# A twelve-stage perceiver block: idle transposes at stage ends, first products by column group, tensors moved in parts, and a new order of rounds in the first cross-attention

## The chip, the cores and the metric

The kernel runs on one core of a Trainium2 chip. The metric is the device time of one execution in microseconds; the kernel before took 2767.07 us as a median of three runs (2764.23 to 2768.42).

## What is computed

The tokens x are 32 sequences of 64 positions with 128 features (2048 rows), the context is 32 sets of 1601 keys with 128 features. Twelve blocks are added to x in turn, each working on the normalised rows of x. The first:

```python
def _L0_xattn_ref(hm_tokens, text_tokens, text_mask, Wq, bq, Wk, bk, Wv, bv):
    Q = hm_tokens @ Wq + bq
    K = text_tokens @ Wk + bk
    V = text_tokens @ Wv + bv
    scores = jnp.einsum('bqd,bkd->bqk', Q, K) / jnp.sqrt(jnp.float32(d))
    scores = jnp.where(text_mask[:, None, :] == 0, jnp.float32(NEG), scores)
    attn = jax.nn.softmax(scores, axis=-1)
    return jnp.einsum('bqk,bkd->bqd', attn, V)
...
    x = x + _L0_xattn_ref(_layernorm(x, axis=-1), ctx_1024, mask_BxS2_ik0, ...)
    x = x + _L0_attn_ref(_layernorm(x, axis=-1), ...)   # and ten more blocks of this form
```

## The kernel before

x stays on the chip the whole time as 16 tiles of 128 rows by 128 features. Every block of the reference is one `Stage`; between two stages all engines meet at a barrier. Before the first there is `start` (L313), which reads x (1 MB, one transfer, L322) and the identity matrix `ident` (L323) and takes the row statistics of the 16 tiles (`measure` L165 with L169, `aggregate` L174 with L179); after the last there is `finish` (L340), which stores x to `out` in one transfer (L348).

**The normalisation.** Nearly every stage begins with the same three helpers. `ln_scalar` (L239) forms the standard deviation (L270); `ln_vector` (L190) its reciprocal (L206) and then the normalised tiles, 11 on VectorE (L213, `VECTOR_TILES` L161) and 5 on ScalarE (L252, `SCALAR_TILES` L162), in four groups of four tiles; the last group has two tiles on each. `ln_tensor` (L293) issues 14 transposes of the identity whose results nobody reads (L303, called idle transposes here) and then four transposes per group (L307), called PT0 to PT3. Their results are copied to `xnT` as four column groups T0 to T3: T0, T1 and T3 by ScalarE (L263), T2 by VectorE (L234). The two psum banks in `tp` alternate, so PT2 waits for T0 and PT3 for T1. The first products of each stage wait for T2 and T3, which means for all four groups.

**The first cross-attention** (`cross_attention`, L352 to L725, used once). SP issues all its transfers in one order: the mask (L428), six small weights (L430, the last, bv, L431), the context of round 0, then it waits until the mask has become additive keys on GpSimd (L486, L487), stores them to `scratch_q`, waits for that store, and reads them back spread over partitions as masks of rounds 0 to 2 (L446), with the contexts of rounds 1 to 3 between. One round r handles two of the 32 sequences: 1.6 MB of context are loaded (L437, L439); TensorE turns them, 26 transposes in 8 units T00 to T13 (L516), the first digit the sequence, the second the group of keys; ScalarE copies the T0 units (L702) and VectorE the T1 units (L641) to `ctxT`, which SP also stores for later stages (`context_turned`, 1.6 MB). The scores S0 to S3 (L540) go through mask and maximum on VectorE (L633, steps s0 to s3), the exponential on ScalarE (L710), four units of transposes of the probabilities p0 to p3 (L529), their copies (L722, and L682 for p3), 52 products with the context, M0 to M3 (L552), then division by the row sum (L660, step o), a transpose (L558, oT), its copy (L667), the product with Wv (L562, out) and the addition to x (L685), after which the tile's statistics for the next stage are taken. Round 0 also makes q (L505), qk (L570) and qbk (L573), and VectorE adds bv to all of x (L653) before it takes s0 of round 0.

The order on TensorE is written out by hand. In a steady round before it is T00 T10 T01, M0 M1 of round r-2, T11 T02 T12, M2 M3, S0, T03 T13, oT, p0 of round r-1, S1 to S3, p1 to p3, out. Three psum banks (`turn`) take the T and p units in turn, so each waits for the copy three units before it; `ctxT` and `sc` have two buffers, `ctx` four, the additive masks three. The fourth cross-attention (`kept_cross_attention`, L3790) is a separate function whose TensorE order has first the turns and then p, M and S of whole rounds.

## Time and profile before

The profiled execution took 2768.07 us; its span, from the first to the last instruction, is 2766.2 us, so 1.9 us lie around it. The mean clock granted to TensorE was 0.944 of full speed.

| stage | lines | from, us | to, us |
|---|---|---|---|
| start | 313 | 0 | 12.0 |
| first cross-attention | 352 | 12.3 | 223.5 |
| spectral | 1447 | 223.8 | 338.8 |
| capacity experts | 1671 | 339.1 | 453.4 |
| causal cross | 727 | 453.7 | 495.7 |
| two-step attention | 1183 | 496.0 | 665.4 |
| routed experts | 1911 | 665.7 | 923.3 |
| many-head cross | 3089 | 923.6 | 2053.1 |
| selective scan | 2166 | 2053.6 | 2311.6 |
| chosen adapters | 2561 | 2311.8 | 2401.6 |
| kept cross | 3790 | 2401.9 | 2569.7 |
| self-attention | 959 | 2570.0 | 2668.0 |
| quantised FFN | 2856 | 2668.3 | 2760.5 |
| finish | 340 | 2760.8 | 2766.2 |

How to read it: the stages follow each other without overlap, so a saving counts where it shortens a stage's longest chain. TensorE has two clock levels here, granted clock 1.0 (2.4 GHz) and 0.5 (1.2 GHz); the 14 idle transposes at a stage's start take 1.72 us at the first and 3.22 us at the second.

### The profile page before, as it was taken

The numbers are of one execution on the slowest core, as the hardware profiler recorded it, in microseconds if no ns is written. First come the engines' busy times: TensorE is split into PE (matmuls) and PEld (weight loads), VectorE is DVE, ScalarE is ACT, GpSimd is POOL, SyncE is SP. The second block draws the span as 40 slices with busy tenths as digits, with TensorE's granted clock in tenths as the row PEclk, the third lists the DMA queues.
The fourth block names the chain that finished last, engine by engine and source line by source line (L and its number), as shares of the span: only waits on it lengthen the run. The fifth ranks groups of instructions, "written<-read, shape, count | busy, mean of one in ns | idle before, by whom it ended". The sixth has DMA issues, their size and how long they took to land. (4 is left out here: it accounts for less than half of the span.)

```text
span 2766.2 us, 74345 instructions
## 1 busy us (share of the span) xinstructions
PE 2520.3 (91%) x31101; PEld 1693.8 (61%) x31101; DVE 1857.7 (67%) x6153; ACT 1385.0 (50%) x2566; POOL 433.1 (16%) x316
## 2 busy tenths in 40 slices
PE   7999844898999999999999999999987998899875
PEld 4776644455777556666666666666654554667544
DVE  5553423676211478888888888888857888466675
ACT  3443312565333245555555555555548994244452
POOL 1000022441000100000000000000002992056410
PEclk9999977998999789999999999999988999999987
DMA  6991041000000100000010000000001220298000
GB/s 213 336 309 36 23 153 41 10 3 18 16 16 16 33 25 26 26 26 26 26 35 29 26 26 26 26 26 26 15 10 57 99 92 16 72 344 285 10 2 16
DMA packets 73373, 181.12 MB, mean 65 GB/s; under 512 B 12130, under 2 KB 39717, under 8 KB 73008
## 3 DMA queue, kind: packets, MB, share of 16 engines
q1 hardware_dynamic: 72016, 174.52, 19.2%
q8 instruction: 247, 4.05, 0.6%
q0 software_dynamic: 1024, 1.85, 0.2%
q14 instruction: 86, 0.70, 0.1%
HBM read 145.80 MB, written 30.79 MB: 64 GB/s over the span
## 5 line engine op out<-in xcount | busy, mean ns | idle before, releaser
L3475 DVE CUSTOM_DVE_ANT_0 L_xattn_junk<-L_xattn_ps_mx,L_xattn_shift 128x512 f32<-128x512 f32 (+1 forms) x1024 | 545.0, 570 | 146.4 <-issue 145.8
L3553 ACT ACTIVATE L_xattn_pT<-L_xattn_ps_st 128x512 f32<-128x512 f32 x768 | 417.0, 595 | 322.6 <-PE L_xattn_ps_st L3290 204.8
L3305 PE MATMUL L_xattn_ps_mx<-L_xattn_kT,L_xattn_qb 32*128 32x512 f32 (+1 forms) x2048 | 530.2, 564 | 0.0
L3290 PE MATMUL L_xattn_ps_st<-L_xattn_qb,L_xattn_kT 32*128 32x256 f32 (+1 forms) x3328 | 462.9, 377 | 0.0
L3513 DVE TENSOR_TENSOR L_xattn_pT<-L_xattn_pT,L_xattn_capT 128x1024 f32<-128x1024 f32 (+1 forms) x324 | 360.1, 1113 | 7.7 <-ACT L_xattn_pT L3553 6.0
L3290 PEld LDWEIGHTS L_xattn_ps_st<-L_xattn_qb,L_xattn_kT 32*128 32x128 f32 (+1 forms) x3328 | 332.8, 181 | 7.1
L3355 PE MATMUL L_xattn_ps_pv<-L_xattn_pT,L_xattn_v 128*17 128x128 f32 x6656 | 261.6, 275 | 0.0
L3355 PEld LDWEIGHTS L_xattn_ps_pv<-L_xattn_pT,L_xattn_v 128*17 128x17 f32 x6656 | 148.6, 96 | 141.6 <-issue 124.5
L3305 PEld LDWEIGHTS L_xattn_ps_mx<-L_xattn_kT,L_xattn_qb 32*128 32x128 f32 x2048 | 176.5, 187 | 25.1 <-DVE L_xattn_tops L3475 18.9
L3317 PE MATMUL L_xattn_ps_st<-L_xattn_less,L_xattn_ones_b 3*128 3x512 bf16 x768 | 177.2, 385 | 0.0
L3228 POOL TENSOR_TENSOR L_xattn_qb<-ln_sq,L_xattn_four 128x256 f32<-128x256 f32 x32 | 20.6, 645 | 998.7 <-PE L_xattn_ps_st L3290 994.2
L2150 ACT ACTIVATE L_ffn_gelu<-L_ffn_ps_h,L_ffn_b 128x512 f32<-128x512 f32 x128 | 87.1, 688 | 130.7 <-PE L_ffn_ps_h L1999 127.4
L2122 DVE SCALAR_TENSOR_TENSOR x<-L_ffn_ps_o,L_ffn_weights,x 128x128 f32<-128x128 f32 x128 | 36.0, 345 | 169.4 <-PE L_ffn_ps_o L2009 169.4
L2009 PEld LDWEIGHTS L_ffn_ps_o<-L_ffn_w,L_ffn_gelu 128*128 128x128 f32 x1024 | 120.8, 194 | 16.6 <-issue 14.1
L3317 PEld LDWEIGHTS L_xattn_ps_st<-L_xattn_less,L_xattn_ones_b 3*128 3x128 bf16 x768 | 51.0, 91 | 130.0 <-ACT L_xattn_pT L3553 69.2
L2009 PE MATMUL L_ffn_ps_o<-L_ffn_w,L_ffn_gelu 128*128 128x128 f32 x1024 | 121.1, 277 | 1.9 <-DVE x L2122 1.9
L3376 PE MATMUL L_xattn_ps_prep<-L_xattn_wv,L_xattn_ctxT 128*32 128x128 f32 (+1 forms) x3264 | 117.8, 278 | 0.0
L1999 PE MATMUL L_ffn_ps_h<-xnT,L_ffn_w 128*128 128x512 f32 x256 | 117.0, 600 | 0.0
L3249 PE MATMUL L_xattn_ps_prep<-L_xattn_ctxT,L_xattn_wk 128*32 128x512 f32 x992 | 108.7, 510 | 0.0
L3887 POOL TENSOR_SCALAR L_xattn_out_keys<-L_xattn_mask 128x1536 bf16<-128x1536 uint8 x16 | 78.8, 4926 | 171.0 <-DMA L_xattn_rest<-context_turned 153.4
L2547 ACT ACTIVATE L_attn_xs<-L_attn_xiT,L_attn_bt 128x256 f32<-128x256 f32 x256 | 105.2, 494 | 0.0
L3376 PEld LDWEIGHTS L_xattn_ps_prep<-L_xattn_wv,L_xattn_ctxT 128*32 128x32 f32 (+1 forms) x3264 | 91.9, 111 | 15.5 <-ACT L_xattn_kT L3566 10.0
(633 smaller groups left out, 4853.9 us busy)
## 6 DMA issues: line engine op xcount, KB each, us to landing
L_xattn_ctx<-in_ctx SPq DMA_DIRECT2D x64, 768.0 KB
context_turned<-L_xattn_ctxT SPq DMA_DIRECT2D x32, 800.5 KB, 9.4
L_xattn_ctxT<-context_turned SPq DMA_DIRECT2D x32, 800.5 KB, 4.4
L_xattn_rest<-context_turned SPq DMA_DIRECT2D x32, 544.5 KB, 9.2
L_attn_cc<-scratch_rows SPq DMA_DIRECT2D x32, 512.0 KB, 3.6
L_xattn_out_keys<-scratch_q SPq DMA_DIRECT2D x32, 200.1 KB, 10.0
L_ffn_w<-in_L_ffn_w SPq DMA_DIRECT2D x4, 1024.0 KB, 9.4
L_ffn_w<-in_L_ffn_W SPq DMA_DIRECT2D x16, 256.0 KB, 3.1
```

What stands on the lines that cost most here:

```text
L1999: nc.tensor.matmul(ph[:, k, :], w1[:, e % 2, P * k:P * k + P], c.xnT[:, 512 * i:512 * i + 512], start=True, stop=True).then_inc(PE.did(f"h ...
L2009: last = nc.tensor.matmul(po[:, n % 2, P * j:P * j + P], g[:, n % 2, k, P * j:P * j + P], w2[:, e % 2, k, :], start=(k == 0), stop=(k == F ...
L2547: last = nc.scalar.mul(xs[:, k % 2, j, :], xiT[:, t, :], bt[:, t, n:n + 1])
L3249: last = nc.tensor.matmul(to[32 * q:32 * q + 32, 0:width], wk[:, 32 * q:32 * q + 32], ctxT[:, n % 2, 512 * m:512 * m + width], start=True, ...
L3290: last = nc.tensor.matmul(st[0:chunk[j], w % 3, 256 * c2:256 * c2 + 256], kT[n % 3][r:r + 32, P * j:P * j + chunk[j]], qb[n % 3][r:r + 32, ...
L3305: last = nc.tensor.matmul(mx[:, w % 3, to:to + width], qb[n % 3][32 * g:32 * g + 32, 2 * (p % 2):2 * (p % 2) + 2, :].rearrange("p h q -> p ...
L3317: nc.tensor.matmul(st[:, w % 3, :], ones_b[r:r + 3, :], less[n % 2][r:r + 3, :, :].rearrange("p c k -> p (c k)"), start=True, stop=False, ...
L3355: last = nc.tensor.matmul(pv[32 * q:32 * q + 17, P * half:P * half + P], v[n % 3][0:chunk[j], j, 4 * half + q, :], pT[b % HELD][0:chunk[j] ...
L3376: last = nc.tensor.matmul(prep[k:k + wide, to:to + P], ctxT[:, n % 2, P * j + k:P * j + k + wide], wv[:, :], start=True, stop=True, tile_p ...
L3475: last = nc.vector.tensor_tensor_reduce(out=junk[:, w % 3, to:to + width], in0=mx[:, w % 3, to:to + width], in1=shift[:, k0:k0 + width], s ...
L3513: nc.vector.tensor_tensor(x, x, capT[0:k, j[0]:j[1], :].unsqueeze(2).broadcast_to([k, j[1] - j[0], 8, S]), ALU.min)\
L3553: nc.scalar.activation(pT[b % HELD][:, :, gi, :], st[:, w % 3, :].rearrange("p (c k) -> p c k", c=2), ACT.Exp)\
```

## The change

1. **Tiles.** Tile 14 is normalised by VectorE and no longer by ScalarE.
2. **Idle transposes at stage ends.** A helper `keep_warm` issues n transposes of the identity on TensorE after a stage's last product: 20 in start (after the identity and the first half of x have landed), 11 in the first cross-attention, 26 in spectral, 30 in capacity (after the last gathered rows have arrived), 30 in causal cross, 11 in two-step, 30 in routed, 34 in the scan, 26 in chosen. The many-head, kept, self and quantised stages get none.
3. **First products by column group.** A helper `turned_group` waits for one of T0 to T3; in the first cross, capacity, routed, two-step, self, scan, chosen and kept stages a product waits for its own group only. In routed the wait for T2 stays in front.
4. **Start.** The identity is read first, then x in two halves with a semaphore each; statistics of half 0 are taken before half 1 is waited for.
5. **Finish** is gone. The quantised stage's SP stores `out` in four parts of 256 KB, each as soon as its group of four tiles is done.
6. **First cross-attention.** GpSimd's mask operation waits for the last normalised group of VectorE. SP issues the contexts of rounds 0 to 2 before the store of the additive keys, then masks 0 to 2, then context 3; in a later round it issues the mask, the turned context of r-2, then the context. `turn` has four banks (the result of the M products moves into the bank `small`), `ctxT` three buffers. A round has two parts: turns T00 T10 T01 T11, oT of r-3, T02 T12 T03 T13, out of r-3, then p0 to p3 of r-2, M0 to M3 of r-2, S0 to S3 of r; rounds run from 0 to 18. VectorE takes max, nmx, bias of r-1 and oT between its copies, and its four mask steps last. ScalarE copies T0 to T3, then p of r-2, then takes the exponential of r-1.

```diff
-VECTOR_TILES = ((0, 1, 2), (4, 5, 6), (8, 9, 10), (12, 13))
-SCALAR_TILES = ((3,), (7,), (11,), (14, 15))
+VECTOR_TILES = ((0, 1, 2), (4, 5, 6), (8, 9, 10), (12, 13, 14))
+SCALAR_TILES = ((3,), (7,), (11,), (15,))
...
+def keep_warm(c, bank, times):
+    for _ in range(times):
+        c.nc.tensor.transpose(bank[:, 0:P], c.ident[:, :], c.ident[:, :])
+def turned_group(pe, V, A, i, tag="ln"):
+    pe.wait_ge(*(V if i == 2 else A).at(f"{tag}_T{i}"))
...
         def _(sp):
-            sp.dma_start(c.x[:, :, :], a["x"].rearrange("(t p) d -> p t d", p=P)).then_inc(loaded, 16)
-            sp.dma_start(c.ident[:, :], a["c_ident"]).then_inc(loaded, 16)
-            sp.wait_ge(loaded, 32)
+            sp.dma_start(c.ident[:, :], a["c_ident"]).then_inc(halves[0], 16)
+            for i in (0, 1):
+                sp.dma_start(c.x[:, 8 * i:8 * i + 8, :], a["x"][8 * P * i:8 * P * i + 8 * P, :].rearrange("(t p) d -> p t d", p=P))\
+                    .then_inc(halves[i], 16)
...
+            pe.wait_ge(halves[0], 32)
+            keep_warm(c, idle, 20)
...
-            dve.wait_ge(loaded, 32)
-            measure(c, dve, *range(NT))
-            aggregate(c, dve, *range(NT))
+            for i in (0, 1):
+                dve.wait_ge(halves[i], 32 - 16 * i)
+                measure(c, dve, *range(8 * i, 8 * i + 8))
+                aggregate(c, dve, *range(8 * i, 8 * i + 8))
...
         def _(sp):
...
-            for r in range(4):
+            for r in range(3):
                 load_context(r)
-                if r == 0 and not indicated:
-                    sp.wait_ge(keys_made, 1)
...
+            sp.wait_ge(keys_made, 1)
+            sp.dma_start(a["scratch_q"][0, 0:B, 0:KEYS], key_out[:, :]).then_inc(keys_moved, 16)
+            sp.wait_ge(keys_moved, 32)
+            for r in range(3):
+                load_mask(r)
+            load_context(3)
...
                 load_mask(r - 1)
+                keep_turned(r - 2)
                 if r < NT:
                     sp.wait_ge(*PE.at(f"M3_{r - 4}"))
                     load_context(r)
...
         def _(pool):
+            pool.wait_ge(keys_moved, 16)
+            pool.wait_ge(*V.at("ln_xn3"))
...
         def _(pe):
             ln_tensor(c, pe, V, A, PE, tp)
             pe.wait_ge(weights, 96)
-            pe.wait_ge(*V.at("ln_T2"))
-            pe.wait_ge(*A.at("ln_T3"))
             for i in range(4):
+                turned_group(pe, V, A, i)
...
                 if g == 0 and r > 0:
-                    pe.wait_ge(*V.at(f"o_{r - 1}"))
+                    pe.wait_ge(*V.at(f"x_{r - 1}"))
...
+            for r in range(NT + 3):
+                scoring, mixing, finishing = r < NT, 2 <= r < NT + 2, r >= 3
                 if scoring:
-                    turn_context(r, 0, 0)
-                    turn_context(r, 1, 0)
-                    turn_context(r, 0, 1)
+                    for t in turned[0:4]:
+                        turn_context(r, int(t[1]), int(t[2]))
                 if finishing:
-                    mix(r - 2, 0)
-                    mix(r - 2, 1)
+                    turn_result(r - 3)
                 if scoring:
+                    for t in turned[4:8]:
+                        turn_context(r, int(t[1]), int(t[2]))
                 if finishing:
+                    project(r - 3)
...
+                if mixing:
+                    for g in range(NG):
+                        turn_probs(r - 2, g)
+                    for g in range(NG):
+                        mix(r - 2, g)
                 if scoring:
+                    for g in range(NG):
+                        score(r, g)
+            keep_warm(c, turn[:, 0, :], 11)
...
+            pe.wait_ge(fetched[1], 128)
+            keep_warm(c, ph[:, 0, :], 30)
...
+        @block.sync
+        def _(sp):
+            for g in range(G):
+                sp.wait_ge(*V.at(f"x_{g}"))
+                sp.dma_start(a["out"][4 * P * g:4 * P * g + 4 * P, :].rearrange("(t p) d -> p t d", p=P), c.x[:, 4 * g:4 * g + 4, :])\
+                    .then_inc(stored, 16)
+            sp.wait_ge(stored, 16 * G)
```

## Rows read from the trace of the kernel before

**Rows 1.** The page, part 1: busy time, share and instructions of each engine.
```profile
PE 2520.3 (91%) x31101; PEld 1693.8 (61%) x31101; DVE 1857.7 (67%) x6153; ACT 1385.0 (50%) x2566; POOL 433.1 (16%) x316
```
**Rows 2.** Windows: length; busy PE, PEld, DVE, ACT, POOL; granted clock; DMA share; GB/s.
```profile
0.00:12.30 12.30, 0.00 (x0) 0.00 (x0) 4.45 (x34) 1.49 (x2) 0.20 (x4) 1.00 0.33 91
12.30:24.00 11.70, 6.95 (x30) 5.98 (x30) 10.13 (x14) 3.97 (x9) 7.28 (x2) 0.90 0.54 187
...
41.00:52.00 11.00, 8.24 (x44) 3.95 (x40) 6.72 (x19) 4.55 (x6) 0.00 (x0) 0.86 0.84 301
52.00:200.00 148.00, 147.78 (x1452) 109.00 (x1451) 85.23 (x342) 67.69 (x119) 0.00 (x0) 1.00 0.95 318
```
**Rows 3.** Timeline of start: start and length in us, idle before and releaser.
```profile
7.62 3.19 DVE L169 BATCH_NORM_STATS2 ln_stats<-x 128x6 f32<-128x128 f32 x16 [6.72 <-DMA ident<-in_c_ident]
10.84 1.17 DVE L179 BATCH_NORM_AGGREGATE ln_mean_var<-ln_stats 128x2 f32<-128x6 f32 x16
```
**Rows 4.** Timeline of the first cross-attention's run-in.
```profile
15.05 0.43 SPq L431 DMA_DIRECT2D L_xattn_bv<-in_L_xattn_bv  x1
...
15.23 6.83 POOL L486 TENSOR_SCALAR L_xattn_key_out<-L_xattn_mask 32x1536 bf16<-32x1536 int32 x1 [14.79 <-DMA L_xattn_mask<-in_mask_keys]
```
**Rows 5.** The same run-in, timeline of TensorE alone.
```profile
24.17 5.82 PE L505 MATMUL L_xattn_ps_scores<-xnT,L_xattn_wq 128*128 128x512 f32 x8 [0.77 <-ACT xnT L263]
29.82 2.99 PE L516 MATMUL L_xattn_ps_turn<-ident,L_xattn_ctx 128*128 128x128 f32 x25
...
40.68 2.80 PE L540 MATMUL L_xattn_ps_scores<-L_xattn_ctxT,xn 128*64 128x512 f32 x12
```
**Rows 6.** One line's instructions, 0 to 40 us: duration min/median/max in ns.
```profile
L213 DVE TENSOR_SCALAR xn<-x,ln_mean_var,ln_rstd x11: 339/342/6817, 13.0 to 20.8; 128x128 f32<-128x128 f32 x11
```
**Rows 7.** The same line in the causal stage, 440 to 480 us.
```profile
L213 DVE TENSOR_SCALAR xn<-x,ln_mean_var,ln_rstd x11: 339/341/344, 454.6 to 457.2; 128x128 f32<-128x128 f32 x11
```
**Rows 8.** DMA issues from 12.3 to 22 us: KB, median us to landing.
```profile
L_xattn_bv<-in_L_xattn_bv SPq DMA_DIRECT2D x1, 64.0 KB, 5.4
```
**Rows 9.** DMA from 37 to 200 us: totals, and one issue.
```profile
DMA packets 12421, 51.65 MB, mean 317 GB/s; under 512 B 1695, under 2 KB 3486, under 8 KB 12402
...
context_turned<-L_xattn_ctxT SPq DMA_DIRECT2D x28, 800.5 KB, 9.4
```
**Rows 10.** Timeline of the kept cross: its last M products.
```profile
2563.76 3.06 PE L3918 MATMUL L_xattn_ps_mixed<-L_xattn_ctx,L_xattn_probsT 128*64 128x128 f32 x52
```
**Rows 11.** Timeline of the start of the capacity stage.
```profile
339.16 3.22 PE L303 MATMUL L_ffn_ps_turn<-ident 128*128 128x128 f32 x14 [3.42 <-PEq L125]
...
346.25 0.92 PE L1772 MATMUL L_ffn_ps_small<-L_ffn_wg,xnT 128*128 128x16 f32 x7 [0.72 <-issue]
```
**Rows 12.** Timeline of the start of self-attention.
```profile
2570.00 1.72 PE L303 MATMUL L_attn_ps_turn<-ident 128*128 128x128 f32 x14 [1.46 <-PEq L125]
...
2575.72 1.52 PE L1059 MATMUL L_attn_ps_misc<-xnT,L_attn_w 128*128 128x512 f32 x3 [0.87 <-ACT xnT L263]
```
**Rows 13.** Windows in the capacity stage; until 390.3 TensorE runs only idle transposes (L1781).
```profile
386.70:390.30 3.60, 3.53 (x17) 3.53 (x18) 0.00 (x0) 0.00 (x0) 0.00 (x0) 0.50 0.70 205
390.30:392.00 1.70, 1.45 (x13) 1.21 (x11) 0.65 (x1) 0.21 (x1) 0.00 (x0) 1.00 0.62 183
```
**Rows 14.** Timelines: the first instructions that wait for a transfer, three stages.
```profile
226.23 0.31 ACT L270 ACTIVATE ln_std<-ln_mean_var,eps_twice 128x16 f32<-128x16 f32 x1 [6.73 <-DMA L_attn_wto<-in_L_attn_W_toT]
...
503.28 0.30 PEld L1289 LDWEIGHTS L_attn_ps_misc<-xnT,L_attn_w 128*128 128x128 f32 x2 [1.08 <-DMA L_attn_shift<-in_c_shift]
...
2320.02 1.96 PE L2630 MATMUL L_ffn_ps_ps<-xnT,L_ffn_wd 128*128 128x512 f32 x4 [1.74 <-DMA L_ffn_diag<-in_c_ident]
```
**Rows 15.** Timeline of the end of the capacity stage.
```profile
448.61 1.14 DVE L1887 SCALAR_TENSOR_TENSOR x<-L_ffn_got,L_ffn_weight,x 128x128 f32<-128x128 f32 x4 [5.60 <-DMA L_ffn_got<-scratch_out,L_ffn_frm]
```
**Rows 16.** Windows: one stretch early in the many-head cross.
```profile
943.30:991.00 47.70, 47.70 (x244) 19.21 (x242) 19.44 (x109) 6.61 (x12) 0.00 (x0) 0.50 0.05 18
```
**Rows 17.** DMA issues at the end, 2755 to 2767 us.
```profile
out<-x SPq DMA_DIRECT2D x1, 1024.0 KB, 5.1
```

More of the change, by code:

```diff
@@ L316, in start @@
         nc, a = c.nc, c.a
-        loaded, eps_set = s.sem("loaded"), s.sem("eps_set")
+        halves, eps_set = [s.sem(f"half{i}") for i in (0, 1)], s.sem("eps_set")
+        idle = s.ps("idle", [P, 512])
         block = s.block()
@@ L360, in cross_attention @@
     wide = [w for _, w in SPANS]
-    indicated = mask_rows != 1
-    UNITS = ["T00", "T10", "T01", "T11", "T02", "T12", "T03", "T13", "p0", "p1", "p2", "p3"]
+    assert mask_rows == 1
+    turned = ["T00", "T10", "T01", "T11", "T02", "T12", "T03", "T13"]
+    turns = [u for r in range(NT + 2) for u in [f"{t}_{r}" for t in turned] * (r < NT) + [f"qk{g}" for g in range(NG)] * (r == 0) +
+             [f"p{g}_{r - 2}" for g in range(NG)] * (r >= 2)]
+    turn_of = {u: n for n, u in enumerate(turns)}
     with Stage(c, name) as s:
@@ new lines, in cross_attention @@
+        v_round = lambda r: (([f"T1{g}_0" for g in range(NG)] + ["qbk", "xbv"] if r == 0 else
+                              [n for g, m in enumerate(("max", "nmx", "bias")) for n in [f"T1{g}_{r}"] * (r < NT) + [f"{m}_{r - 1}"] * (r <= NT) + [f"oT_{r - 3}"] * (r >= 3 and g == 1)] +
+                              [f"T13_{r}"] * (r < NT)) +
+                             [f"x_{r - 3}"] * (r >= 3) + [f"p3_{r - 2}"] * (2 <= r < NT + 2) +
+                             [f"rinv_{r - 2}", f"o_{r - 2}"] * (2 <= r < NT + 2) + [f"s{g}_{r}" for g in range(NG)] * (r < NT))
@@ L530, in turn_probs @@
                                                c.ident[:, :])
-                last.then_inc(PE.did(f"{unit}_{r}"), 1)
+                last.then_inc(PE.did(unit), 1)
             def score(r, g):
@@ L572, in _ @@
-            for t in range(NT):
-                last = nc.tensor.matmul(small[:, t:t + 1], qT[:, P * t:P * t + P], bk[:, :], start=True, stop=True)
-            last.then_inc(PE.did("qbk"), 1)
-            pe.wait_ge(*A.at("qk3"))
-            for g in range(NG):
-                score(0, g)
-            for r in range(1, NT + 2):
-                scoring, using, finishing = r < NT, r <= NT, r >= 2
+            for r in range(NT + 3):
+                scoring, mixing, finishing = r < NT, 2 <= r < NT + 2, r >= 3
@@ L856, in _ @@
             result(3)
+            keep_warm(c, tp[0], 30)
         @block.vector
@@ L1340, in _ @@
                     late(unit)
+            keep_warm(c, h.turn[:, 0, :], 11)
         @block.vector
@@ L1572, in _ @@
             out(3)
+            keep_warm(c, tp[0], 26)
         @block.vector
@@ L2038, in _ @@
                 second(n)
+            keep_warm(c, ph[:, 0, :], 30)
         @block.vector
@@ L2371, in _ @@
             out(3)
+            keep_warm(c, ps[:, 0, :], 34)
         @block.gpsimd
@@ L2691, in _ @@
             up(3)
+            keep_warm(c, ps[:, 0, :], 26)
         @block.vector
```

331 lines of the change are left out of this document (132 added, 199 removed).

## Prediction

> **What bounds the kernel now.** I read the page's busy times first: TensorE is busy for 2520.3 us of 2766.2, in 31101 matmuls [rows 1]. The windows of the first cross-attention say the same more sharply: from 52 to 200 us TensorE is busy for 147.78 of 148.00 us at full clock while the DMA engines are at 0.95 [rows 2]. A new order of the same products can't shorten such rounds. What is left to gain lies at the borders: between stages, where the clock is at 0.5 and TensorE waits for the normalisation; in the run-ins; at the first load and the last store. So I read, in this order, the timeline of start and of the first run-in [rows 3 to 8], the DMA of the rounds [rows 9], the starts of the other stages [rows 11, 12, 14], and the end [rows 17]. The sum is made against the profiled run, 2768.07 us, which is 1.0 above the median of 2767.07.
>
> **Start and the run-in of the first cross-attention.** VectorE begins the 16 statistics at 7.62, when the identity, issued last, has landed; they and the aggregates take 3.19 and 1.17 us [rows 3]. With two halves only the second half's work, 2.2 us, stands behind the last landing: -2.15 us (bounds -1.3, if the second transfer lands later than both did, to -2.5). The 20 idle transposes run in TensorE's idle time, which is the whole of start [rows 2]; they cost nothing unless they last beyond VectorE.
>
> The GpSimd mask operation takes 6.83 us from 15.23 [rows 4], and one of VectorE's normalised tiles takes 6817 ns beside it [rows 6] where it takes 339 to 344 in a stage without that operation [rows 7]. That is 6.48 us, and TensorE's q products at 24.17 [rows 5] stand behind it. The Trainium skill ("SBUF — State Buffer", section "SBUF: two separate sides") says that VectorE and GpSimd share a port pair as an exclusive lock for a whole instruction; the trace agrees (6817 ns beside 6.83 us). After the change the mask operation waits for VectorE's last group, and q could start at 24.17 - 2.15 - 6.48 = 15.5. It won't: q needs the weights too, and bv is issued at 15.05 [rows 4] and lands 5.4 us later [rows 8], so at 15.05 - 2.15 + 5.4 = 18.3. The eight products took 5.82 us, partly at half clock [rows 5]; TensorE idles before them again, so I take half clock for most of them and the first turn of round 0 at 23.5 instead of 29.82 [rows 5]: -6.3 us (bounds 22.0 and 24.2; the 1.6 MB of the first context need 5.2 us at the rounds' 317 GB/s [rows 9], from 18.3 to 23.5, which is the same).
>
> From there to the last scores. In 41 to 52 us TensorE was idle for 2.76 us (11.00 less 8.24) and a mean clock of 0.86 took another 1.5 [rows 2]: VectorE's addition of bv and the masks held the first scores (40.68 [rows 5]). The new order puts the turns of two more rounds before it needs probabilities, so I let nearly all of that vanish: -3.8 (bounds 0 and -4.3). The masks are the risk here: they now stand behind three contexts (4.9 MB, 15.5 us at 317 GB/s, so 34 us), and round 0's scores need them at 34.8 to 37; a late mask costs up to 2 us, inside the bounds. The mask operation itself (6.83, now from about 15.5) ends by 22.8 and hides behind those contexts. The 13 steady rounds stay as they are, at zero. The tail grows: the last-but-one M products, 3.06 us in the kept stage's like order [rows 10], now stand behind the last scores, +2.6 after some overlap (bounds +2 and +3.1). Eleven idle transposes end beside the last copy, product and statistics on VectorE: 0. Together -6.3 - 3.8 + 2.6 = **-7.5 us** for start and first cross (bounds -4 and -10).
>
> **Idle transposes at the other borders.** A stage now starts with 14 idle transposes in 3.22 us at half clock [rows 11]; self-attention, whose start is at full clock, takes 1.72 [rows 12]. From these to the first product are 7.09 us in the one and 5.72 in the other. If the clock is held over the border by `keep_warm`, 1.4 us of the ln chain go; the wait per column group and the tile moved off ScalarE take about another 1.0, as the first product needs T0 alone. A stage that waits for nothing else gains up to 2.4. But a transfer often comes last [rows 14]:
> - spectral: the standard deviation waits for a transfer at 226.23, 2.4 us after the stage began, so only what follows shortens: -0.8 (0 to -1.3).
> - capacity: first logits 346.25 [rows 11], nothing late in the way: -2.6. But its `keep_warm` (30) waits for the gathered rows that arrive at 448.61 [rows 15], after a long idle, so 30 x 3.22/14 = 6.9 us at most and 6.4 by my count from 448.7 on, against VectorE's end at 453.4: up to +1.7 at the end of the stage; I take +0.9. Net -1.7.
> - causal: its 1.6 MB key loads come last whatever TensorE does: 0.
> - two-step: its product starts at 503.28 on a transfer [rows 14]: -0.4, and its 11 idle transposes may run at half clock beyond VectorE's end: +0.7. Net +0.3 (-0.5 to +1.5).
> - routed, many-head and scan: partly on weights, read the same way: -1.0 each (0 to -2.5).
> - chosen: the products wait for a transfer at 2320.02 [rows 14]. TensorE's normalisation ends sooner while this doesn't, the idle time before it grows from 1.7 to 3.6 us, and the clock may fall under the products: +1.5 (0 to +2.5).
> - kept: its queries come sooner, the first context doesn't: +0.3 (0 to +1.5).
> - self: no `keep_warm` before it, its clock was high anyway; a shorter wait at 2575.72 [rows 12], but the chance that the start falls to half clock, 1.5 to 2 us: +1.0.
> - quantised: bound by VectorE, which has one tile (0.34 us) more [rows 7]: +0.25.
>
> A rule that speaks against all of this: the Trainium skill ("TensorE: Matmul & The Clock Gate", section "Part 4: PE-mode transpose") says that full clock doesn't engage for transposes. The trace disagrees: from 386.7 to 390.3 TensorE runs only transposes of the identity at 0.50, and from 390.3 on the clock is 1.00 [rows 13]. By the rule the borders would gain what the second rival gives.
>
> **The end.** `out` takes 5.1 us from issue to landing for 1 MB [rows 17]. Of that 3.3 are data at 317 GB/s [rows 9] and 1.8 fixed; the last quarter needs 1.8 + 0.8 = 2.6. So -2.5, and -0.3 for the barrier of a stage that is gone: **-2.8** (-2.3 to -3.3). The other three quarters are hidden behind products on a queue that is nearly empty there.
>
> **Sum.** -7.5 - 0.8 - 1.7 + 0.3 - 1 - 1 - 1 + 1.5 + 0.3 + 1 + 0.25 - 2.8 = -12.45, so 2755.6 against the profiled run and **2754.6** against the median.
>
> **Rivals.**
> *The borders give nothing* (the change doesn't do what it says). Transfers anchored to the stage's start come last, and where TensorE has to wait for them the clock falls again. Only start, run-in and the store remain: -6.5 there, -1.6 from the waits per group, +4.75 of the costs above, -2.8: -6.2, **2761**. For it: three anchors in rows 14. Against: four stages have none.
> *A long stretch at half clock goes.* In the many-head cross TensorE is busy for all of 943.3 to 991 and yet at 0.50 [rows 16]; it costs some 24 us. The change shifts what comes before it by a microsecond, and if the clock's fall at 943.3 depends on that, most of it may go: -12.5 - 17 gives **2738**. It might as well stay or be joined by another; nothing in the rows says which.
> *The first cross keeps its time.* Contexts and masks land behind one another so that round 0 starts sooner but rounds 1 to 3 wait: its -7.5 shrinks to +0.5, **2763**.
> *Slower: DMA becomes the bound of the rounds.* In 37 to 200 us 51.65 MB move, 317 GB/s [rows 9], at a share of 0.95 [rows 2]; a turned store takes 9.4 us to land. If the new order of SP, with the stores ahead of the context, brings the rate under 283 GB/s, the 11.1 us rounds become 12.5 and 13 of them cost 18 us, which is more than everything else gives; at 280 GB/s: **2775**. Against: the bytes are the same, and three `ctxT` buffers and four contexts give more room than before.
>
> **Chances.** About 0.2%, 5.5 us, is what a measurement of this kernel can tell from no change. Forecast 0.60 (own range 2747 to 2761); borders give nothing 0.18; the long stretch 0.10; the first cross keeps its time 0.07; DMA-bound 0.05. Faster (under 2761.5): 0.56 + 0.09 + 0.10 = 0.75; within: 0.04 + 0.09 + 0.07 = 0.20; slower (over 2772.6): 0.05. The range 2741 to 2764 leaves out most of the long-stretch case and of the slower one.
>
> **What would show it.** Right: the statistics of x in two groups and start over near 9.9; no tile of L213 over 0.4 us; q at 18 to 19; T_0 of round 0 at 22 to 24.2; steady rounds at 11.1 us; capacity's first logits within 5 us of its start; no clock fall over the border where the next stage isn't held by a transfer; the span ending 2.6 us after the last part is issued. Wrong: q waiting for the mask's port again; a wait of VectorE for mask 0; rounds longer than 11.2 with TensorE waiting for context; idle transposes that end after VectorE's last statistics; half clock under the products of chosen, kept or self for longer than counted.

## The result, and the profile after

The changed kernel takes 2732.88 us as a median of four executions (2726.26 to 2750.17) against 2766.97 for the kernel before: -34.1 us, a ratio of 0.9888 with a 95% interval of 0.9842 to 0.9934. It is faster, as forecast, but by nearly three times the forecast 12.45 us, and below the range (2741 to 2764). Its four times also spread over 24 us where the four of before spread over 4. The profiled execution took 2732.19 us, its span is 2730.4.

The page's first part, beside rows 1:

```profile
PE 2505.5 (92%) x31289; PEld 1702.8 (62%) x31319; DVE 1850.1 (68%) x6165; ACT 1379.5 (51%) x2554; POOL 434.4 (16%) x316
```

The page counts 188 matmuls more. The change adds 218 idle transposes; the other 30 are records that are missing from this trace (of the 64 products with the causal and the strict mask in two-step, whose code is unchanged, it holds 34). TensorE is busy for 14.8 us less all the same: the same products took less time. Stage by stage, from the first instruction of a stage's normalisation on TensorE to that of the next (the last column is the forecast):

| stage | before, us | after, us | difference | forecast |
|---|---|---|---|---|
| start and first cross | 223.9 | 211.2 | -12.6 | -7.5 |
| spectral | 115.3 | 115.8 | +0.5 | -0.8 |
| capacity | 114.6 | 114.4 | -0.2 | -1.7 |
| causal | 42.3 | 42.1 | -0.2 | 0 |
| two-step | 169.7 | 172.2 | +2.4 | +0.3 |
| routed | 257.9 | 257.5 | -0.4 | -1.0 |
| many-head | 1130.0 | 1118.9 | -11.1 | -1.0 |
| scan | 258.3 | 253.2 | -5.1 | -1.0 |
| chosen | 90.1 | 91.2 | +1.1 | +1.5 |
| kept | 168.1 | 167.6 | -0.4 | +0.3 |
| self, quantised, store | 196.2 | 186.3 | -9.9 | -1.5 |

Half of the gain stands where the change touches little: in many-head, and at the end beyond the store. First the part that it does touch. The windows of the first cross-attention after, with the columns of rows 2:

```profile
10.40:22.00 11.60, 7.83 (x36) 4.82 (x37) 5.90 (x21) 3.61 (x8) 6.98 (x2) 0.89 0.64 212
...
39.80:52.00 12.20, 12.06 (x111) 9.62 (x110) 8.52 (x34) 9.22 (x15) 0.00 (x0) 1.00 1.03 383
52.00:188.00 136.00, 135.11 (x1394) 107.43 (x1391) 79.20 (x329) 63.39 (x114) 0.00 (x0) 1.00 0.98 339
```

The timeline of its run-in, beside rows 3 and 5:

```profile
8.31 1.61 DVE L169 BATCH_NORM_STATS2 ln_stats<-x 128x6 f32<-128x128 f32 x8
...
18.35 5.40 PE L488 MATMUL L_xattn_ps_scores<-xnT,L_xattn_wq 128*128 128x512 f32 x8 [2.84 <-DMA L_xattn_bv<-in_L_xattn_bv]
23.58 2.97 PE L499 MATMUL L_xattn_ps_turn<-ident,L_xattn_ctx 128*128 128x128 f32 x26
...
34.39 5.59 PE L520 MATMUL L_xattn_ps_scores<-L_xattn_ctxT,xn 128*64 128x512 f32 x16
```

The products q wait for bv and start at 18.35 (18.3 forecast), the first turn at 23.58 (23.5), the first scores at 34.39. The rounds are where it differs. TensorE's timeline of one round before, from the first scores of one round to the last M product of the next:

```profile
84.52 1.03 PE L540 MATMUL L_xattn_ps_scores<-L_xattn_ctxT,xn 128*64 128x512 f32 x4
85.48 0.34 PE L516 MATMUL L_xattn_ps_turn<-ident,L_xattn_ctx 65*128 65x65 f32 x2
85.65 0.28 PE L558 MATMUL L_xattn_ps_small<-ident,L_xattn_o 128*128 128x128 f32 x1
85.77 0.60 PE L529 MATMUL L_xattn_ps_turn<-ident,L_xattn_sc 128*128 128x128 f32 x4
86.30 2.06 PE L540 MATMUL L_xattn_ps_scores<-L_xattn_ctxT,xn 128*64 128x512 f32 x12
88.28 1.21 PE L529 MATMUL L_xattn_ps_turn<-ident,L_xattn_sc 128*128 128x128 f32 x9
89.32 0.39 PE L562 MATMUL L_xattn_ps_small<-L_xattn_wv,L_xattn_oT 128*128 128x128 f32 x2
89.71 1.50 PE L516 MATMUL L_xattn_ps_turn<-ident,L_xattn_ctx 128*128 128x128 f32 x12
91.14 1.97 PE L552 MATMUL L_xattn_ps_mixed<-L_xattn_ctx,L_xattn_probsT 128*64 128x128 f32 x32
93.03 1.53 PE L516 MATMUL L_xattn_ps_turn<-ident,L_xattn_ctx 128*128 128x128 f32 x12
94.50 1.31 PE L552 MATMUL L_xattn_ps_mixed<-L_xattn_ctx,L_xattn_probsT 128*64 128x128 f32 x20
```

And one after, with the next round's first scores:

```profile
64.05 2.87 PE L520 MATMUL L_xattn_ps_scores<-L_xattn_ctxT,xn 128*64 128x512 f32 x16
66.84 1.97 PE L499 MATMUL L_xattn_ps_turn<-ident,L_xattn_ctx 128*128 128x128 f32 x16
68.65 0.27 PE L538 MATMUL L_xattn_ps_small<-ident,L_xattn_o 128*128 128x128 f32 x1
68.76 1.16 PE L499 MATMUL L_xattn_ps_turn<-ident,L_xattn_ctx 128*128 128x128 f32 x10
69.91 0.49 PE L542 MATMUL L_xattn_ps_small<-L_xattn_wv,L_xattn_oT 128*128 128x128 f32 x2
70.24 1.60 PE L509 MATMUL L_xattn_ps_turn<-ident,L_xattn_sc 128*128 128x128 f32 x13
71.77 3.06 PE L532 MATMUL L_xattn_ps_small<-L_xattn_ctx,L_xattn_probsT 128*64 128x128 f32 x52
74.66 0.60 PE L520 MATMUL L_xattn_ps_scores<-L_xattn_ctxT,xn 128*64 128x512 f32 x2
```

26 turns, 13 probability turns, 52 M products, 16 matmuls of scores, and one round is 11.12 us before and 74.66 - 64.05 = 10.61 after (nine of its 13 steady rounds; the other four are 10.7 to 11.1, so the 13 together take 139.2 us instead of 144.6). In both TensorE shows no idle time. Turns, M products and scores alternate: nine changes of kind a round before, five after (a turn, oT and p are one kind). Counted by the form in these rows, transposes (most of them `128*128`) against scores and M products (both `128*64`), it is six changes before and two after.

Now the many-head cross. Windows of its run-in after, the third being what answers to rows 16:

```profile
913.10:932.70 19.60, 15.73 (x88) 7.00 (x88) 12.23 (x32) 6.99 (x15) 11.33 (x13) 1.00 0.37 114
932.70:944.40 11.70, 11.70 (x111) 5.59 (x110) 7.80 (x35) 2.14 (x5) 0.00 (x0) 1.00 0.01 2
944.40:968.30 23.90, 23.90 (x122) 9.32 (x122) 10.26 (x66) 3.65 (x7) 0.00 (x0) 0.50 0.11 35
```

The stretch at half clock is 23.9 us long and begins 31.3 us into the stage; before it was 47.7 us and began at 19.7. The 23.8 us at half clock that are gone are worth some 12 us (an estimate: half of them).

The end, beside rows 17, on SP's timeline and then in the list of DMA issues:

```profile
2727.70 0.37 SPq L2959 DMA_DIRECT2D out<-x  x1
```
```profile
out<-x SPq DMA_DIRECT2D x1, 256.0 KB, 2.3
```

From the last x (2727.7) to the end are 2.7 us instead of 5.7: -3.0, where -2.8 was forecast.

### The profile page after: what moved, and what is told of

Read it like the earlier page. It is cut to its first block and busy times, and to the rows that moved or that the text cites. A ratio compares the mean times of both kernels' runs of the same rounds, so it can differ in the third digit from the quotient of the medians.

```text
span 2730.4 us, 74764 instructions
## 1 busy us (share of the span) xinstructions
PE 2505.5 (92%) x31289; PEld 1702.8 (62%) x31319; DVE 1850.1 (68%) x6165; ACT 1379.5 (51%) x2554; POOL 434.4 (16%) x316
## 5 line engine op out<-in xcount | busy, mean ns | idle before, releaser
L3290 PE MATMUL L_xattn_ps_mx<-L_xattn_kT,L_xattn_qb 32*128 32x512 f32 (+1 forms) x2048 | 524.3, 557 | 0.0
```

What stands on the lines that cost most here:

```text
L3290: last = nc.tensor.matmul(mx[:, w % 3, to:to + width], qb[n % 3][32 * g:32 * g + 32, 2 * (p % 2):2 * (p % 2) + 2, :].rearrange("p h q -> p ...
```

## The experiments

"Many-head" below is that stage's length in the profile of each kernel.

| kernel | median, us | times, us | ratio to before (95%) | many-head, us |
|---|---|---|---|---|
| changed | 2732.9 | 2726 to 2750 | 0.9842 to 0.9934 | 1118.9 |
| e1, changed again | 2737.2 | 2720 to 2749 | 0.9847 to 0.9950 | 1121.2 |
| e3, first cross alone | 2754.7 | 2752 to 2758 | 0.9933 to 0.9976 | 1130.1 |
| e4, no idle transposes at ends | 2729.7 | 2725 to 2741 | 0.9856 to 0.9919 | 1118.5 |
| e12, the same | 2731.2 | 2714 to 2743 | 0.9855 to 0.9890 | 1111.1 |
| e8, tile alone | 2762.0 | 2744 to 2769 | 0.9954 to 1.0004 | 1131.6 |
| e9, tile back | 2745.1 | 2744 to 2754 | 0.9909 to 0.9956 | 1131.6 |
| e7, four idle in many-head | 2724.3 | 2722 to 2728 | 0.9835 to 0.9867 | 1111.9 |
| e16, the same | 2727.6 | 2723 to 2729 | 0.9840 to 0.9871 | 1112.0 |
| e10, four in every bundle, no ends | 2725.1 | 2721 to 2728 | 0.9832 to 0.9863 | 1115.6 |
| e14, before with the four | 2745.9 | 2740 to 2754 | 0.9915 to 0.9947 | 1109.4 |
| e15, and start and store | 2744.5 | 2742 to 2750 | 0.9912 to 0.9938 | 1112.0 |
| e17, as e7, none in start | 2723.0 | 2723 to 2730 | 0.9830 to 0.9861 | 1112.1 |
| e13, as e7, none at ends | 2722.2 | 2713 to 2725 | 0.9816 to 0.9848 | 1112.0 |
| e18, the same | 2719.3 | 2715 to 2729 | 0.9811 to 0.9857 | 1112.2 |

e2, e5, e6 and e11 were timed once, at 2767.0, 2745.8, 2757.4 and 2750.9. The kernel before ran 56 times beside all of these: 2760.0 to 2776.4, median 2766.9.

**Is it chance?** e1 is the changed kernel, e2 the kernel before, unedited. The expectations weigh two theories of the gain in the many-head stage. Theory A: when the clock falls there is chance in part, so the stretch at half clock has another length in each execution and the times spread by it, while the other stages repeat. Theory B: the shorter stretch belongs to the change and stays as it is.

> The changed kernel once more. [...] Theory B (the gain there belongs to the change): the stretch is again 24 us long, and the time 2733 within 3 us.

> The kernel before once more, for its second profile. Theory A: its stretch at half clock in the many-head run-in (943.3 to 991.0) changes its length too, from 24 to 48 us. Theory B: it is there with the same 47.7 us, as its four times agree within 4 us. Rounds of the first cross-attention 11.12 us either way.

e1: first cross ending at 209.3, rounds 10.62, many-head with 30.7 us at half clock from 30.5 on, times from 2720 to 2749. e2: 47.8 us from 19.3 on, a time of 2767.03. So theory A holds for the changed kernel. It was wrong of the kernel before: in both of its profiles the stretch is there and as long. The granted clock of each execution says the same: 0.948 to 0.962 as a mean over the changed kernel's eight executions, its slowest (2750.2 us) having the lowest and its fastest (2720.0) the highest.

**The first cross alone**, the new function put into the kernel before:

```diff
-        turn = s.ps("turn", [P, 3, 512])
+        turn = s.ps("turn", [P, 4, 512])
...
-            for r in range(1, NT + 2):
-                scoring, using, finishing = r < NT, r <= NT, r >= 2
+            for r in range(NT + 3):
+                scoring, mixing, finishing = r < NT, 2 <= r < NT + 2, r >= 3
...
```

> The kernel before with the new first cross-attention alone (orders, banks, buffers, mask behind the normalisation, products per group), without its idle transposes at the end; start, other stages, tiles and finish as before. If the order of kinds on TensorE makes the round, its rounds take 10.62 us and the stage is 10.5 to 11.5 us shorter than the 211.5 of before. If start's idle transposes and the warm entry carry a part, the stage gains under 9. Many-head run-in: Theory A, its low stretch changes with a shift of 11 us alone; Theory B (the gain comes from the warm entry after routed), it stays 47.7 us. Time: 2756 by B, 2730 to 2756 by A.

The stage is 198.2 us instead of 211.5 (-13.4, more than the 11.5 expected), the rounds 10.62. Two of them are longer, 10.98 and 10.99. Many-head keeps its 47.8 us and its 1130 us, the time is 2754.7. This part is a gain of its own, and it doesn't move the stretch.

**Without idle transposes at stage ends:**

```diff
 def keep_warm(c, bank, times):
-    for _ in range(times):
-        c.nc.tensor.transpose(bank[:, 0:P], c.ident[:, :], c.ident[:, :])
+    return
```

> The changed kernel without any of the idle transposes at stage ends (keep_warm issues nothing). My forecast said that they bring the many-head, routed, capacity and scan stages 1 us each and cost chosen and the tails some; the profile of after shows those stages at -0.2 to +2.4 us, so I now expect the stages to change by less than 1.5 us each without them, two-step's +2.4 to go if its 11 idle transposes cause it, and the starts of stages to show 3.22 us for their first 14 transposes again. Theory B: the low stretch of the many-head run-in returns to 47.7 us and the time to 2745 to 2755. Theory A: it takes any of its lengths.

> The changed kernel without idle transposes at stage ends, once more, for more times. Its four so far were 2724.9 to 2741.3, those of the changed kernel 2720.0 to 2750.2 in eight. If they bring nothing, both have their means within 5 us of each other; if they cost what its stages show (two-step, kept, capacity, causal, spectral together some 5 us), this one's mean stays 3 to 6 us lower, near 2731; if they hold the clock, it is above 2737.

Ten times of e4 and e12 have a mean of 2730.8, eight of the changed kernel 2735.7; they spread over 28 and 30 us, so this difference isn't clear of chance. Most stages start with about 3.2 us for 14 transposes again and are no longer for it: two-step is 169.2 and 168.5, kept 165.4 and 167.4, causal 41.1 and 41.8 in e4 and e12, against 172.2, 167.6 and 42.1. Many-head has a stretch of 23.9 us at half clock in e4. In e12 the long stretch is absent: only the first 9.0 us of the stage are at half clock.

**The tile**, the only thing that was then common to the kernels with the shorter stretch:

```diff
-VECTOR_TILES = ((0, 1, 2), (4, 5, 6), (8, 9, 10), (12, 13))
-SCALAR_TILES = ((3,), (7,), (11,), (14, 15))
+VECTOR_TILES = ((0, 1, 2), (4, 5, 6), (8, 9, 10), (12, 13, 14))
+SCALAR_TILES = ((3,), (7,), (11,), (15,))
```

> The kernel before with nothing but tile 14 moved from ScalarE to VectorE. In the profiles so far the many-head run-in has its 47.8 us at half clock, from 19.3 to 19.6 us after the stage's start, in all three kernels with the old tiles, and only 24 to 31 us, from 30.5 to 31.3 us on, in all three with the new ones, with or without idle transposes. Theory C (the tile sets it): here many-head is 1118 to 1121 us instead of 1130, scan 253 instead of 258, the time 2748 to 2754. Theory D (it takes the tile together with an entry shifted or warm by another part): many-head stays at 1130, time 2767.

> The changed kernel with tile 14 back on ScalarE and all else as changed. Theory C: many-head is 1130 us again with 47.8 us at half clock, scan 258, the time 2750 to 2756. Theory D: many-head stays below 1122 and the time near 2735.

Both show 51.2 us at half clock. Theory C is gone: the tile alone leaves the profile's stretch where it was. Yet two of its ten times are 2744.4 and 2744.6 and the other eight 2759 to 2769, and e9's are 2743.7 to 2753.5: with one small move the kernel has two kinds of execution, and the two fast ones have the highest granted clocks of the ten (0.952 and 0.954; the others 0.941 to 0.950). In both, scan is 255.1 us instead of 258.3.

**What makes the round?** The same products with four changes of kind more, and with three psum banks for the turns.

```diff
                 if mixing:
-                    for g in range(NG):
+                    for g in (0, 1, 2):
                         turn_probs(r - 2, g)
-                    for g in range(NG):
-                        mix(r - 2, g)
+                    mix(r - 2, 0)
+                    turn_probs(r - 2, 3)
+                    mix(r - 2, 1)
                 if scoring:
-                    for g in range(NG):
+                    score(r, 0)
+                if mixing:
+                    mix(r - 2, 2)
+                    mix(r - 2, 3)
+                if scoring:
+                    for g in (1, 2, 3):
                         score(r, g)
```

> The changed kernel with the same products of the first cross-attention in an order that changes kind four times more per round: p0 p1 p2, M0, p3, M1, S0, M2 M3, S1 to S3. Theory S (each change of kind on TensorE costs about 0.07 to 0.1 us, although TensorE shows busy through it): rounds of 10.62 + 4 x 0.08 = 10.9 to 11.05 us, the stage 4 to 6 us longer. Theory W (before's longer rounds came from waits for psum banks or for o, not from changes of kind): rounds stay at 10.62.

```diff
-        turn = s.ps("turn", [P, 4, 512])
+        turn = s.ps("turn", [P, 3, 512])
...
-            before = turns[turn_of[unit] - 4]
+            before = turns[turn_of[unit] - 3]
```

> The changed kernel with three psum banks for the turns instead of four, all else as changed. Four more changes of kind cost 0.29 us a round, so they explain 0.29 of the 0.50 us by which the rounds became shorter. If the rest is the fourth bank, rounds take 10.8 here; if it is the order (a copy less waited for), they stay at 10.62 to 10.65.

e5's rounds are 10.91 us: 0.29 for four changes, 0.073 each as a mean. Its timeline, through the part that differs:

```profile
59.13 1.09 PE L532 MATMUL L_xattn_ps_small<-L_xattn_ctx,L_xattn_probsT 128*64 128x128 f32 x16
60.16 0.33 PE L509 MATMUL L_xattn_ps_turn<-ident,L_xattn_sc 128*65 128x128 f32 x1
60.41 1.09 PE L532 MATMUL L_xattn_ps_small<-L_xattn_ctx,L_xattn_probsT 128*64 128x128 f32 x16
61.34 1.03 PE L520 MATMUL L_xattn_ps_scores<-L_xattn_ctxT,xn 128*64 128x512 f32 x4
```

From start to start, 16 M products take 1.03 us where a transpose follows (59.13 to 60.16) and 0.93 where scores follow (60.41 to 61.34), and the one transpose takes 0.25 where most follow each other by 0.11. So the four changes aren't alike: the two between transposes and M products carry nearly all of the 0.29, the two between M products and scores next to nothing. By changes of form, after has two a round, e5 four and before six: 0.29 us for two is 0.145 each, and 0.50 for four is 0.125 each. One price of 0.13 to 0.15 us fits all three rounds. It is read off them; no run was made to test it.

e11's rounds are 11.16, more than expected and as long as before. Where it goes is in its timeline, beside the round after:

```profile
68.63 1.12 PE L499 MATMUL L_xattn_ps_turn<-ident,L_xattn_ctx 128*128 128x128 f32 x9
69.91 0.28 PE L499 MATMUL L_xattn_ps_turn<-ident,L_xattn_ctx 65*128 65x65 f32 x1 [0.16 <-ACT L_xattn_ctxT L670]
70.02 0.44 PE L542 MATMUL L_xattn_ps_small<-L_xattn_wv,L_xattn_oT 128*128 128x128 f32 x2
70.54 1.69 PE L509 MATMUL L_xattn_ps_turn<-ident,L_xattn_sc 128*128 128x128 f32 x13
```

From the second turns to the p units are 70.54 - 68.63 = 1.91 us, against 70.24 - 68.76 = 1.48 after: 0.43 of the 0.54 us. The turns wait for the copy three units before them. So the two-part order needs the fourth bank; with both, the round is 0.5 us shorter than before. Whether the order of before would have gained from a fourth bank alone was not run.

**The mask at once:**

```diff
             pool.wait_ge(keys_moved, 16)
-            pool.wait_ge(*V.at("ln_xn3"))
```

> The changed kernel with GpSimd's mask operation started as soon as the mask has landed, as before. If it holds VectorE's port, one of the normalised tiles takes some 6.8 us again instead of 0.34, q starts at 21.5 to 22.5 us instead of 18.35, and the first turn of round 0 at 26.5 to 28 instead of 23.6, the stage is 3 to 4.5 us longer. If the weights were the true limit in both, nothing moves by more than 0.5 us.

The normalisation's line in this kernel (its instructions' min/median/max in ns), and q on TensorE's timeline:

```profile
L226 DVE TENSOR_SCALAR xn<-x,ln_mean_var,ln_rstd x12: 329/340/6792, 11.1 to 20.2; 128x128 f32<-128x128 f32 x12
```
```profile
21.46 5.01 PE L487 MATMUL L_xattn_ps_scores<-xnT,L_xattn_wq 128*128 128x512 f32 x8
```

6792 ns beside the GpSimd operation, where the changed kernel's largest is 345; q at 21.46, the first turn at 26.30, 2.7 us later. That much was expected. But the stage is 199.9 us, against 200.3 and 198.9 in the changed kernel's two profiles. The first scores of rounds 0 and 1 start at 36.5 and 43.1, in the changed kernel at 34.4 and 42.9 with 6.8 us at half clock between 33.0 and 39.8, in e1 at 34.7 and 41.9. The delay shrinks within two rounds, to 1.2 us at most against these two; the price of 3 to 4.5 us was wrong (one execution, in which no round is longer than 10.62). The exclusive lock that the Trainium skill describes ("SBUF — State Buffer", section "SBUF: two separate sides") is seen again; what it costs is what the chain behind it leaves of it.

**Holding the clock** in the many-head run-in, first on the changed kernel, then in all bundles without idle transposes at ends:

```diff
                 if b < 0 and not early(b) and not late(b) and b != CAP_TURNED:
-                    for _ in range(2):
+                    for _ in range(4):
                         nc.tensor.transpose(st[:, 2, 0:P], c.ident[:, :], c.ident[:, :])
```

> The changed kernel with 4 instead of 2 idle transposes in each of the nine idle places of the many-head run-in (18 more, 1.9 us at full clock). Theory C (the tile) fell: the alone-moved tile and three changed kernels showed 51 to 55 us at half clock from 20.2 us on. What is left is theory A: the stretch comes by how the chip's looks fall on a thinly filled instruction stream. If so, fuller TensorE work there holds the clock, many-head is 1108 us in every execution and the spread of the times shrinks to under 8 us around 2723. If the idle transposes don't count as work for the clock, many-head is 2 to 4 us longer than it was (1121 to 1135), the time 2737 to 2748.

> The changed kernel without idle transposes at stage ends, but with 4 in each of the 20 bundles of the many-head run-in (62 more than before, 6.6 us at full clock). Theory A: no low stretch there, many-head 1113 us, times around 2722 to 2726 and within 10 us of each other. If transposes don't count: 1125 to 1140, time over 2737.

Windows of the same part of the stage in e6, then e12, then e7:

```profile
932.20:986.80 54.60, 54.60 (x301) 24.15 (x299) 21.35 (x116) 9.36 (x17) 0.00 (x0) 0.50 0.05 16
```
```profile
920.30:970.00 49.70, 49.15 (x600) 27.51 (x601) 36.07 (x165) 19.08 (x36) 0.00 (x0) 1.00 0.06 18
```
```profile
925.60:974.00 48.40, 47.85 (x584) 27.55 (x585) 35.84 (x166) 17.91 (x34) 0.00 (x0) 1.00 0.06 19
```

e6 and e12 have the same code there: e6 gets through 301 matmuls in its window, at 0.50 with TensorE busy throughout, e12 through 600 in its own, at 1.00. The expectations count nine idle places in the run-in and 18 idle transposes more; the trace has seven places and 14 more:

```profile
L3390 PE MATMUL L_xattn_ps_st<-ident x14: 272/328/476, 929.0 to 955.2; 128*128 128x128 f32 x14
```
```profile
L3390 PE MATMUL L_xattn_ps_st<-ident x28: 272/273/332, 923.9 to 945.9; 128*128 128x128 f32 x28
```

The first is the changed kernel, the second e7 (min/median/max in ns). With these 14 the clock stays at 1.00, many-head is 1111.9 us, and nine times of e7 and e16 lie within 2721.8 and 2729.4, where the changed kernel's eight went from 2720.0 to 2750.2. By the rule of the Trainium skill weighed in the prediction ("TensorE: Matmul & The Clock Gate", section "Part 4: PE-mode transpose") these transposes shouldn't count; here they decide. None of the eight profiles with four in each place has the long stretch, and of the twelve with two only e12's lacks it. Whether they work as activity or by moving what follows them was not separated. e10 has 64 in 16 places (50 more than the changed kernel, where its expectation counts 62) and pays for them without gain: many-head takes 1115.6 us.

**The change's own worth, with the stretch held off.** e14 is the kernel before with the four idle transposes, e15 that with the new start and the store in parts, e16 is e7 again, e13 is e7 without idle transposes at stage ends.

> No idle transposes at stage ends, 4 instead of 2 in the nine idle places of the many-head run-in: the held clock there takes the largest part of the chance away, so the ends can be priced. If the idle transposes at stage ends cost what the stage tables say (about 4 to 6 us together), this is at 2718 to 2721 against 2724 for the same kernel with them. If they are worth nothing and cost nothing, 2722 to 2726. If they pay (my forecast's term, some -3 us after their costs), 2727.

> The kernel before with those four idle transposes in the many-head run-in and nothing else of the change. Theory A: its 47.8 us at half clock go, many-head falls from 1130 to 1107 to 1112 us, the time from 2767 to 2744 to 2750. If the long stretch is held off only by what the change does elsewhere, it stays at 2765 to 2769.

> The one before, and also start with x in halves and its 20 idle transposes, and the result stored in four parts. The traces say -1.5 to -1.9 us for start and -3.0 for the store: 4.5 to 5 us under the kernel with the four idle transposes alone. If start's gain is eaten by the first cross's run-in (weights and mask), only 3.

> The changed kernel with the four idle transposes once more, beside the others of this call, as the base to compare them with: 2722 to 2726, its times within 8 us of each other. Against the kernel before with the four alone, it shows what the change gives when the many-head stretch is out of play: by the stage tables 12.5 (start and first cross) + 3 (store) + 2 to 6 (scan, quantised stage) = 18 to 22 us; by my forecast's sum 12.5.

e14 gains 21.1 us with one edited number, in the kernel before (median 2766.98 beside it): its window of the many-head run-in, 47 us from the start of the stage, is

```profile
925.00:972.00 47.00, 44.53 (x339) 22.28 (x340) 30.98 (x136) 14.25 (x29) 11.27 (x13) 0.97 0.22 66
```

e16 is 18.3 us below e14: the change's own gain (13.5 in their two profiled executions, of which e14's was faster than its median and e16's slower). e13 is 5.4 us below e16: the idle transposes at stage ends cost. Of e15's expected 4.5 us only 1.4 is seen, within the spread of the times. In its profile start is 1.7 us shorter and q starts 1.7 us sooner (22.49 against 24.22), but q takes 6.31 us there against 5.05, and start and first cross together end level (222.8 and 222.6 us).

**The idle transposes of start:**

```diff
-        @block.tensor
-        def _(pe):
-            pe.wait_ge(halves[0], 32)
-            keep_warm(c, idle, 20)
```

> The changed kernel with the four idle transposes in the many-head run-in, and without the 20 in start alone. In all four profiles without idle transposes in start, q takes 3.70 us at full clock and the first scores start at 32.0 to 33.0 us; in the five with them TensorE is through the normalisation early, is idle for 2.4 to 3.8 us until bv lands, and q takes 5.4 to 6.8 us, the first scores starting at 33 to 34.7. If the 20 in start cause that, q takes 3.70 us here and the first cross ends 1 to 2 us sooner, the time 2722 to 2726; if the other stages' idle transposes are behind it, q stays at 5.4 or more.

> The fastest kernel so far once more (no idle transposes at stage ends, four in the many-head run-in): 2718 to 2724 again, and by 0 to 4 us faster than the one beside it, if the other eight stage ends' idle transposes cost something too.

q on TensorE's timeline in e17, then e18, then the changed kernel's second profile, e1:

```profile
17.66 3.70 PE L482 MATMUL L_xattn_ps_scores<-xnT,L_xattn_wq 128*128 128x512 f32 x8 [0.87 <-DMA L_xattn_bv<-in_L_xattn_bv]
```
```profile
18.72 5.40 PE L487 MATMUL L_xattn_ps_scores<-xnT,L_xattn_wq 128*128 128x512 f32 x8 [2.55 <-DMA L_xattn_bv<-in_L_xattn_bv]
```
```profile
17.70 6.76 PE L488 MATMUL L_xattn_ps_scores<-xnT,L_xattn_wq 128*128 128x512 f32 x8 [2.72 <-DMA L_xattn_bv<-in_L_xattn_bv]
```

Taken away alone, they give q its 3.70 us back (e17), as in five other profiles without them (e3, e4, e10, e12, e13; idle time before q at most 1.90 us). The first cross then ends at 209.0 us, against 209.4 in e7 and 211.3 in e16. e18 has none either and takes 5.40: bv landed later there and TensorE had been idle for 2.55 us. So it doesn't look like the transposes as such, but like the idle time between the normalisation and bv, which they lengthen; that rests on e18's one profile. The kernel of e13 and e18 is the fastest found: ten times with a mean of 2720.4 against 2725.9 for the nine of e7 and e16, 46 us below the kernel before.

## Why the prediction was right or wrong

- **The run-in of the first cross: right** up to the first scores, to 0.1 us in q's start, the first turn and the first scores. From there to the scores of round 2 the gain is 2.5 us (19.0 for 21.6), where -3.8 was forecast. What the port was argued to be worth was too much: by e6 the port costs the stage at most 1.2 us against the changed kernel's profiles, although it delays the first turn by 2.7.
- **"The 13 steady rounds stay as they are, at zero": the step that failed** for the first cross. It was read from 147.78 of 148.00 us busy, with the conclusion that a new order of the same products can't shorten them. But busy isn't at its peak: an undisturbed round became 0.5 us shorter, the 13 together 5.4 us in this profile, and the stage beat its forecast by 5.1. What costs, by e5, is changing between transposes and the other products, 0.13 to 0.15 us each time; e11 shows that the order alone, with three banks, gives nothing. The tail grew by less than the +2.6 forecast: from the start of the last scores to the next stage it is 211.2 - 192.6 = 18.6 us, against 223.9 - 206.9 = 17.0 before.
- **Start: right in its own stage** (-1.4 us here, -1.6 to -2.0 in the other profiles, -2.15 forecast), **wrong in "they cost nothing"** of the 20 idle transposes: a wait follows them, and under part of q the clock is at half.
- **The idle transposes at the other borders: the term has the wrong sign.** The clock was held over most of the borders behind them, as forecast, and 14 transposes took 1.72 us there (2.71 in routed). But the stages didn't end sooner, and all `keep_warm` together cost 5.4 us (e13 against e16; 5.4 between the means of ten and nine times). The rival that they are worth nothing had 0.18 and was nearer than the forecast. The profiles show where most of it is: in means over the nine with them and the five of the changed kernel without, chosen takes 92.8 against 90.6 us and two-step 171.3 against 169.8, and the first cross ends at 210.4 (after, e1, e7, e9, e16) against 208.5. For chosen +1.5 was forecast, which fits.
- **The long stretch: the mechanism was the second rival's, and the sum left it at a chance of 0.10.** It was priced as a move from 48 us at half clock to few. In truth it is 24 and 31 us in the changed kernel's two profiles, absent to 55 us in those of its variants with the same many-head code, and 48 in all three profiles with the tiles and the borders of before (before, e2, e3). Some 16 of the 34 us are of this kind, by an estimate: 34.1 less the 18.3 that e16 and e14 show; with the stretch held off on both sides the change gives 18.3, not the forecast 12.45. The range should have held it: this is the second step that failed, a term put at nothing in the sum although its row was at hand. What a row shows as 24 us lost while TensorE is busy throughout can go by a small shift, and nothing in the trace bounded when. Where the prediction says that by the Trainium skill's rule the borders would gain "what the second rival gives", it is the first of its rivals that is meant; and that rival's costs add up to 4.65 us, not 4.75.
- **The store: right** (-3.0 for -2.8). The slower rival, rounds bound by DMA: wrong, the rate rose to 339 GB/s. A few rounds of some profiles are 10.7 to 11.7 us long while most are 10.62; whether DMA holds these was not tried.

Open: why small moves elsewhere let the stretch go in some executions when the fastest of the kernel before's 56 executions took 2759.98 us; and why scan is 3 us shorter with the tile moved alone, also 3 with the tile back and all else changed, and 4 to 5 with both (the idle transposes aren't behind it: its mean is 254.0 us with them and without). The surplus at the end (self, quantised and store together -9.9, of which 3.0 are the store) goes with 35.0 us at half clock there instead of 54.9. e2, e3 and e14, which change nothing in these stages, are 193.6, 194.0 and 190.4 us long there instead of 196.2 (e14 with 38.0 us at half clock), so much of the surplus lay in the profile of before.

## What to carry to other kernels

A busy engine can still be slow: count how often TensorE changes between transposes and other products in a round and how many psum banks lie between a unit and its copy, and compare with another stage that has the same products in another order. Where the granted clock is at half while TensorE is busy, try a few more idle transposes there before anything else (14 of them brought 21 us here); judge it by the spread of the times as well as by the median. Where a wait comes anyway, making TensorE ready earlier gains nothing and can cost: here q took 5.40 us after 2.35 us of idle time (e7) and 3.70 after 0.87 (e17).

## What was not expected of the hardware

- The same part of the program had 55 us at half clock in one profile and no such stretch in another (e6, e12, whose kernels differ only elsewhere), and eight executions of the changed kernel spread over 30 us, at mean granted clocks of 0.948 to 0.962. In the eight profiles with 14 or 50 idle transposes more, of about 0.11 us each, it doesn't come.
- A change between transposes and scores or M products costs 0.13 to 0.15 us, though TensorE shows busy through it; a change between M products and scores costs next to nothing (e5, and the rounds of before and after).
- Where bv comes last, the eight products of q take 3.70 us after 0.86 to 1.90 us without work on TensorE (e13, e3) and 5.27 to 6.76 us after 2.35 or more (e9, e7, e1).
